# Weight quantisation and part of the row norm of a feed-forward placed inside the last units of the attention before it

## What is computed

```python
x = x + tanh(g_xattn[0]) * L0_xattn(ctx_1024, layernorm(x), mask, ...)   # latents attend to context and themselves
x = x + tanh(g_ffn[0])   * L0_ffn(layernorm(x), ...)                     # eight experts, two per row
x = x + tanh(g_xattn[1]) * L1_xattn(layernorm(x), ctx_1024, ...)         # 16 heads of 16
x = x + tanh(g_ffn[1])   * L1_ffn(layernorm(x), w_gate, w_up, w_down)
```

```python
def _weight_quant(w):
    scale = 1.0 / clip(mean(abs(w)), 1e-05)
    return clip(round(w * scale), -1.0, 1.0) / scale
def _act_quant(x):
    scale = 127.0 / clip(max(abs(x), axis=-1), 1e-05)
    return clip(round(x * scale), -128.0, 127.0) / scale
def _bitlinear(x, w):
    return einsum('bsi,oi->bso', _act_quant(x), _weight_quant(w))
def L1_ffn(x, w_gate, w_up, w_down):
    return _bitlinear(silu(_bitlinear(x, w_gate)) * _bitlinear(x, w_up), w_down)
```

## Time and profile before

| | |
|---|---|
| median of 3 runs | 3298.25 us (3297.76 to 3301.66) |
| profiled execution | 3298.45 us |
| its span in the trace | 3296.6 us |
| TensorE (PE) busy | 2955.8 us, 90% |
| VectorE (DVE) busy | 2432.6 us, 74% |
| ScalarE (ACT) busy | 1802.2 us, 55% |
| GpSimd (POOL) busy | 2106.7 us, 64% |
| mean granted TensorE clock | 0.968 |

### The profile page before, as it was taken

How to read it: one execution, slowest core, us unless ns; L and a number is a source line. 1 busy time by engine, 2 the same in 40 slices (tenths; PEclk the granted TensorE clock), 3 DMA queues, 4 the chain that set the end, 5 groups by cost and what they waited for, 6 DMA issues and landing times. The chain is left out here.

```text
span 3296.6 us, 53602 instructions
## 1 busy us (share of the span) xinstructions
PE 2955.8 (90%) x21720; PEld 1092.9 (33%) x21720; DVE 2432.6 (74%) x3016; ACT 1802.2 (55%) x2008; POOL 2106.7 (64%) x1000
## 2 busy tenths in 40 slices
PE   5899999999999999999999999996695899999947
PEld 3233333333333333333333333332562233332314
DVE  8777877677777678767777777872556888888658
ACT  4455455555455555545544554444442788888833
POOL 4787988898898888889789888898500211111022
PEclk9999999999999999999999999998897899999969
DMA  1000000000000000000000000000200100000000
GB/s 61 6 1 1 1 7 1 1 7 1 1 7 1 1 1 7 1 1 7 1 1 2 1 1 1 1 1 1 83 16 13 44 7 8 7 6 7 4 1 26
DMA packets 24616, 28.73 MB, mean 9 GB/s; under 512 B 6511, under 2 KB 21296, under 8 KB 24370
## 3 DMA queue, kind: packets, MB, share of 16 engines
q1 hardware_dynamic: 24370, 25.31, 2.6%
HBM read 17.42 MB, written 2.10 MB: 6 GB/s over the span
## 5 line engine op out<-in xcount | busy, mean ns | idle before, releaser
L460 POOL TENSOR_TENSOR a_acc<-a_acc,a_prob 128x1024 f32<-128x1024 f32 x704 | 1724.7, 2450 | 298.3 <-ACT a_prob L592 216.4
L710 DVE TENSOR_REDUCE a_part_max<-wide 128x2 f32<-128x1024 f32 x880 | 1069.3, 1215 | 442.1 <-PE wide L997 441.4
L592 ACT ACTIVATE a_prob<-slot,a_mask_bias 128x1024 f32<-128x1024 f32 x928 | 987.6, 1113 | 738.4 <-PE slot L1026 721.5
L1041 PE MATMUL bank<-a_prob,a_val 128*64 128x512 f32 x3712 | 896.8, 605 | 2.1 <-ACT a_prob L592 2.1
L1325 ACT ACTIVATE a_prob<-slot,a_mask_bias 128x1024 f32<-128x1024 f32 x416 | 455.4, 1116 | 66.7 <-PE slot L1483 53.7
L997 PE MATMUL wide<-a_k_hi,a_q_hi 64*128 64x512 f16 (+1 forms) x2016 | 352.6, 362 | 113.8 <-DVE a_part_max L710 106.1
L1367 DVE TENSOR_REDUCE a_part_max<-wide 128x1 f32<-128x512 f32 x514 | 333.3, 683 | 37.5 <-PE wide L1471 20.6
L1041 PEld LDWEIGHTS bank<-a_prob,a_val 128*64 128x64 f32 x3712 | 226.4, 136 | 393.7 <-issue 289.2
L1026 PE MATMUL slot<-a_q_hi,a_k_lo 64*128 64x512 f16 x1856 | 352.6, 377 | 0.0
L1026 PE MATMUL slot<-a_q_hi,a_k_step_hi 64*128 64x512 f16 x1728 | 328.1, 376 | 2.3 <-ACT a_prob L592 2.2
L1026 PE MATMUL slot<-a_q_lo,a_k_step_hi 64*128 64x512 f16 x1728 | 327.7, 376 | 0.0
(11 more groups left out here) (391 smaller groups left out, 3277.8 us busy)
## 6 DMA issues: line engine op xcount, KB each, us to landing
a_w_staged<-in_w SPq DMA_DIRECT2D x8, 384.0 KB, 3.2
x_res<-in_x SPq DMA_DIRECT2D x4, 512.0 KB, 5.7
a_q_op<-a_hi SPq DMA_DIRECT2D x128, 16.0 KB, 1.8
out_x<-x_res SPq DMA_DIRECT2D x16, 128.0 KB
a_k_op<-mid_k_hi SPq DMA_DIRECT2D x32, 52.0 KB, 2.2
mid_context<-in_ctxt SPq DMA_DIRECT2D x1, 1601.0 KB, 6.5
mid_w_staged<-in_w1a SPq DMA_DIRECT2D x4, 384.5 KB, 6.3
a_acc<-in_ctx SPq DMA_DIRECT2D x3, 512.0 KB, 8.3
```

The costliest lines, as they stand in the source:

```text
L460: nc.gpsimd.tensor_tensor(acc, before, prob[:, k % R, :], ALU.add).then_inc(added_p, 1)
L592: nc.scalar.activation(prob[:, k % R, :], m.slot[k % 2][:, :], ACT.Exp, bias=mbias[:, t:t + 1]).then_inc(probs_ready, 1)
L710: nc.vector.reduce_max(part_max[:, w % 2, :, j, c], pairs, AX.X).then_inc(max_used, 1)
L1041: ins = nc.tensor.matmul(av[r, :], val[g % 2][:, t, r], prob[:, k % R, h * QB:(h + 1) * QB], start=(t == 0), stop=(t == NT - 1), tile_posi ...
```

## The change

The stage of the row norm is gone, and `stage_norm` with it. `keep_for_quantised` reserves the feed-forward's tiles ahead of the second attention, and `stage_cross` gets them as `ffn`. On VectorE the sums over the weights stand at step 23 of unit 14; the scales and the first weight's quantisation at step 6 of unit 15; the other two at step 12; the measuring of row tiles 0 to 7 at step 18. Behind the last step VectorE measures tiles 8 to 11 and normalises tiles 0 to 11 ahead of `invert(last)`, and takes their row scales behind `divide(last)`. ScalarE takes the square root ahead of `take_raw(last)`. TensorE has the matmul for the mean at step 6 of unit 15. Tiles 12 to 15, those of the last block, are measured, normalised and scaled in the feed-forward's stage, on VectorE around `take_x(0)` and `take_x(1)`. GpSimd there starts without a wait. The normalised tiles 0 to 11 lie in the memory of the context's transposes (`m.ch`, `m.cl`), which nobody reads by then.

```diff
+        self.sum_at, self.mean_at, self.weights_at, self.rows_at = 23, 6, 12, 18
...
+                if w == a.units - 1 and s == a.mean_at:
+                    uses.append(("mean", 0))
...
+            act.wait_ge(rows_measured, 2)
+            deviate_rows(nc, ffn, 0, ffn.early).then_inc(rows_std, 1)
             take_raw(last)
...
+            def weight_sums():
+                dve.wait_ge(fetched, 16 * len(ahead_of_use))
+                nc.vector.memset(ffn.ones[:, :], 1.0)
+                nc.vector.memset(ffn.eps[:, :], EPS)
+                for n in range(3):
+                    ins = nc.vector.tensor_reduce(ffn.wsum[:, n:n + 1], ffn.wf[n][:, :], AX.X, ALU.add, apply_absolute_value=True)
+                ins.then_inc(wsum_done, 1)
+
+            def weight_scales():
+                dve.wait_ge(ring_ready, use_n["mean", 0] + 1)
+                nc.vector.tensor_scalar(ffn.wmean[:, :], bank(("mean", 0))[:, 0:3], 1.0 / (FF * D), 1e-5, ALU.mult, ALU.max).then_inc(ring_used, 1)
+                dve.wait_ge(ring_used, use_n["mean", 0] + 1)
+                nc.vector.tensor_scalar(ffn.gain[:, :], ffn.wmean[:, 2:3], m.tg[:, ffn.gate:ffn.gate + 1], None, ALU.mult)
+                link(nc.vector.reciprocal(ffn.wscale[:, :], ffn.wmean[:, :]))
...
+                    if w == last - 1 and s == a.sum_at:
+                        weight_sums()
+                    if w == last and s == a.mean_at:
+                        weight_scales()
+                        quantise_weight(nc, ffn, 0, link)
+                    if w == last and s == a.weights_at:
+                        quantise_weight(nc, ffn, 1, link)
+                        quantise_weight(nc, ffn, 2, link)
+                    if w == last and s == a.rows_at:
+                        dve.wait_ge(res_added, 2 * (last - 1))
+                        measure_rows(nc, m, ffn, 0, 8, link).then_inc(rows_measured, 1)
+            dve.wait_ge(res_added, 2 * last)
+            measure_rows(nc, m, ffn, 8, ffn.early - 8, link).then_inc(rows_measured, 1)
+            dve.wait_ge(rows_measured, 2)
+            dve.wait_ge(rows_std, 1)
+            norm_rows(nc, m, ffn, 0, ffn.early, link)
             invert(last)
             divide(last)
+            scale_rows(nc, ffn, 0, ffn.early, link).then_inc(rows_scaled, 1)
+            dve.wait_ge(rows_scaled, 1)
...
+            def mean():
+                free_bank(("mean", 0))
+                pe.wait_ge(wsum_done, 1)
+                nc.tensor.matmul(bank(("mean", 0))[:, 0:3], ffn.ones[:, :], ffn.wsum[:, :], start=True, stop=True).then_inc(ring_ready, 1)
...
+                    if w == last and s == a.mean_at:
+                        mean()
...
+    early = [part[:, :, :].rearrange("p c k -> p (c k)").bitcast(FP32) for part in (m.ch, m.cl)]
+    q.xn = [early[t // 6][:, t % 6 * D:(t % 6 + 1) * D] for t in range(NX - 4)]
...
+    q.early = NX - 4
...
+def quantise_weight(nc, q, n, link):
+    w = q.wf[n][:, :]
+    link(nc.vector.tensor_scalar(w, w, q.wscale[:, n:n + 1], ROUND, ALU.mult, ALU.add))
+    link(nc.vector.tensor_scalar(w, w, ROUND, 1.0, ALU.subtract, ALU.min))
+    link(nc.vector.tensor_scalar(q.wq[n][:, :], w, -1.0, None, ALU.max))
...
+def measure_rows(nc, m, q, t0, n, link):
+    for t in range(t0, t0 + n):
+        ins = nc.vector.bn_stats(q.stats[:, t, :], m.x[:, t, :])
+    link(ins)
+    for t in range(t0, t0 + n):
+        ins = nc.vector.bn_aggr(q.mv[:, t, :], q.stats[:, t, :])
+    return ins
+
+
+def deviate_rows(nc, q, t0, n):
+    return nc.scalar.activation(q.std[:, t0:t0 + n], q.mv[:, t0:t0 + n, 1], ACT.Sqrt, bias=q.eps[:, 0:1])
...
+def norm_rows(nc, m, q, t0, n, link):
+    link(nc.vector.reciprocal(q.rstd[:, t0:t0 + n], q.std[:, t0:t0 + n]))
+    for t in range(t0, t0 + n):
+        ins = nc.vector.tensor_scalar(q.xn[t], m.x[:, t, :], q.mv[:, t, 0:1], q.rstd[:, t:t + 1], ALU.subtract, ALU.mult)
+    link(ins)
...
+def scale_rows(nc, q, t0, n, link):
+
+    r = slice(t0, t0 + n)
+    for t in range(t0, t0 + n):
+        ins = nc.vector.tensor_reduce(q.amax[:, t:t + 1], q.xn[t], AX.X, ALU.max, apply_absolute_value=True)
+    link(ins)
+    link(nc.vector.tensor_scalar(q.amax[:, r], q.amax[:, r], 1e-5, None, ALU.max))
+    link(nc.vector.reciprocal(q.ascale[:, r], q.amax[:, r]))
+    nc.vector.tensor_scalar(q.ascale[:, r], q.ascale[:, r], 127.0, None, ALU.mult)
+    link(nc.vector.tensor_scalar(q.adq[:, r], q.amax[:, r], 1.0 / 127.0, None, ALU.mult))
+    nc.vector.tensor_scalar(q.gs[:, r], q.adq[:, r], q.wmean[:, 0:1], None, ALU.mult)
+    return nc.vector.tensor_scalar(q.us[:, r], q.adq[:, r], q.wmean[:, 1:2], None, ALU.mult)
...
-            nc.vector.memset(ones[:, :], 1.0)
-            for n in range(3):
-                ins = nc.vector.tensor_reduce(wsum[:, n:n + 1], wf[n][:, :], AX.X, ALU.add, apply_absolute_value=True)
...
+            measure_rows(nc, m, q, q.early, NX - q.early, link).then_inc(late_measured, 1)
             take_x(0)
             take_x(1)
+            dve.wait_ge(late_std, 1)
+            norm_rows(nc, m, q, q.early, NX - q.early, link)
+            scale_rows(nc, q, q.early, NX - q.early, link).then_inc(rows_ready, 1)
+            dve.wait_ge(rows_ready, 1)
...
-            pool.wait_ge(scales_ready, 1)
             for t in range(NX):
                 if t >= 2:
...
+                if t == q.early:
+                    pool.wait_ge(rows_ready, 1)
+                nc.gpsimd.tensor_scalar(xi[:, t % 2, :], q.xn[t], q.ascale[:, t:t + 1], ROUND, ALU.mult, ALU.add).then_inc(xi_part, 1)
...
-            act.wait_ge(scales_ready, 1)
+            act.wait_ge(late_measured, 1)
+            deviate_rows(nc, q, q.early, NX - q.early).then_inc(late_std, 1)
...
-            pe.wait_ge(wsum_done, 1)
-            nc.tensor.matmul(m.bank[0][:, 0:3], ones[:, :], wsum[:, :], start=True, stop=True).then_inc(wmean_done, 1)
...
-                        pe.wait_ge(wq_done, n + 1)
-                    else:
+                    if t:
...
+            ffn = keep_for_quantised(nc, m, ctx)
...
-            with nc.sbuf_tensor("xn_rows", [P, NX, D], FP32) as rows:
-                stage_norm(nc, m, "nx3", m.x, NX, rows=rows)
-                stage_quantised(nc, m, rows, 3, wf, out)
...
+            stage_quantised(nc, m, ffn, out)
```

More of the change, by code:

```diff
@@ L2135, in _, with keep_for_quantised, sb @@
                 turn(1, b)
-def stage_quantised(nc, m, xn, gate, wf, out):
+def keep_for_quantised(nc, m, ctx):
+    def sb(name, shape, dt=FP32):
+        return ctx.enter_context(nc.sbuf_tensor(f"ffn_{name}", shape, dt))
+    q = Memory()
+    q.gate = 3
+    q.wf = [sb(f"w{n}", [P, FF * DC]) for n in range(3)]
+    q.wq = [sb(f"wq{n}", [P, FF * DC], BF16) for n in range(3)]
+    q.ones = sb("ones", [P, P])
+    early = [part[:, :, :].rearrange("p c k -> p (c k)").bitcast(FP32) for part in (m.ch, m.cl)]
+    q.xn = [early[t // 6][:, t % 6 * D:(t % 6 + 1) * D] for t in range(NX - 4)]
+    q.wsum, q.wmean, q.wscale, q.gain = sb("wsum", [P, 3]), sb("wmean", [P, 3]), sb("wscale", [P, 3]), sb("gain", [P, 1])
+    q.stats, q.mv, q.std, q.rstd, q.eps = sb("stats", [P, NX, 6]), sb("mv", [P, NX, 2]), sb("std", [P, NX]), sb("rstd", [P, NX]), sb("eps", [P, 1])
+    q.amax, q.ascale, q.adq = sb("amax", [P, NX]), sb("ascale", [P, NX]), sb("adq", [P, NX])
+    q.gs, q.us = sb("gate_scale", [P, NX]), sb("up_scale", [P, NX])
+    q.early = NX - 4
+    return q
@@ L2143, in stage_quantised @@
+def stage_quantised(nc, m, q, out):
     KF = FF // P
@@ L2146, in sb @@
             return ctx.enter_context(nc.sbuf_tensor(f"ffn_{name}", shape, dt))
-        wq = [sb(f"wq{n}", [P, 2048], BF16) for n in range(3)]
-        ones = sb("ones", [P, P])
-        wsum, wmean, wscale = sb("wsum", [P, 3]), sb("wmean", [P, 3]), sb("wscale", [P, 3])
-        amax, ascale, adq = sb("amax", [P, NX]), sb("ascale", [P, NX]), sb("adq", [P, NX])
-        gain = sb("gain", [P, 1])
-        gs, us = sb("gate_scale", [P, NX]), sb("up_scale", [P, NX])
+        wq = q.wq
+        late = sb("xn", [P, 4, D])
+        q.xn += [late[:, t, :] for t in range(4)]
         xi = sb("xi", [P, 2, D])
@@ L2255, in _ @@
         def _(act):
[L2256 removed]
+            act.wait_ge(late_measured, 1)
+            deviate_rows(nc, q, q.early, NX - q.early).then_inc(late_std, 1)
             for t in range(NX):
                 act.wait_ge(gate_ready, t + 1)
+                if t == q.early:
+                    act.wait_ge(rows_ready, 1)
                 if t >= 2:
                     act.wait_ge(h_done, t - 1)
[L2261 removed]
+                nc.scalar.activation(sg[:, t % 2, :], m.slot[0][:, :], ACT.Silu, scale=q.gs[:, t:t + 1]).then_inc(silu_done, 1)
                 if t:
```

148 lines of the change are left out of this document (17 added, 131 removed).

## The result

The changed kernel takes **3268.87 us** (median of 4 runs, 3268.37 to 3270.92), against 3298.72 for the kernel before in runs that alternate with it. The ratio is 0.9911, 95% interval 0.9900 to 0.9923: 29.9 us less. The forecast was 3266.8 in a range of 3263 to 3271.

What follows compares the result with a forecast made beforehand. VectorE was taken to bound the last feed-forward loop and to work nearly alone before it; h of tile 0 moving from 3204.83 to 3173.15 saves 31.7 us, so 3298.45 becomes 3266.8, range 3263 to 3271.

Steps and rivals of the forecast that it cites:

- Sums, mean, first weight: hidden.: Last attention units: weight sums, mean matmul and first weight's passes fit idle time at cost 0, reciprocal spare about 0.1 us.
- The other weights, the measuring: hidden.: Last attention unit: second and third weight (8.1 us) and measuring rows 0 to 11 end before ScalarE's last exponential, hidden.
- Deviation +0.43: End of attention: square root with table load on ScalarE delays the copy of the last values by 0.43 us.
- Normalising ahead of the last reciprocal +2.93: End of attention: twelve normalisations on VectorE delay the last softmax's reciprocal by 2.93 us, the deviation's 0.43 included.
- The clock falls before the spread.: TensorE idles before the last spread and drops to 1.2 GHz: spread to division about 2.05 us, outputs 3.7.
- Stage end.: Attention's end: GpSimd ends last near 3163.4 (+5.3 us), hiding VectorE's row scales at 3162.7; next stage starts at 3164.4.
- h of tile 0: First product of the feed-forward's last loop, expected at 3173.15 instead of 3204.83, set by VectorE's row scales.
- my rival of chance 0.06: New stage: VectorE's late normalisations wait for GpSimd on tile 2, +0.95 us, so 3267.7; chance 0.06.
- My other road, through Silu: New stage: gate matmuls, then 4.5 us to Silu's end, table load included, 8.35 us behind the stage's start.
- The loop unchanged.: Feed-forward's last sixteen-tile loop, VectorE's: untouched by the change, still 5.3 us a tile.
- The clock rises later in the loop: Rival: 3 to 7 us more at 1.2 GHz slow tiles 0 to 2, giving 3267.5 to 3271; chance 0.06.
- the held softmax: Rival: first weight's passes delay unit 14's reciprocal, TensorE stands at the spread; 3267.6 to 3269.4; chance 0.12.

Runs made afterwards that it cites:

- fill_gap: Changed kernel plus twelve matmuls without use in TensorE's idle time between the last denominators and the spread; 3266.99 us.
- weights_only: Changed kernel with only the weights' sums and quantisation left in the attention, all sixteen row tiles back in the feed-forward's stage; 3281.06 us.
- norm_split_fill: Changed kernel with the twelve normalisations split in fours around last reciprocal and division, plus matmuls without use in TensorE's waits of tiles 0 and 1; 3263.23 us.
- after_again: The changed kernel run and profiled a second time with no edit; median 3270.00 us.
- after: First profile of the changed kernel, no further edit; median 3268.87 us.
- after_third: Third profile of the changed kernel, no edit; a single execution of 3268.49 us.
- invert_first: Changed kernel with VectorE's last reciprocal and division ahead of the norm of row tiles 0 to 11; 3271.20 us.

## Why the prediction was right

Step by step, against the changed kernel's profile:

- **Sums, mean, first weight: hidden.** Right. The mean fitted TensorE's gap (the scores behind it start 11.01 us behind the mark, before 11.02), and the reciprocal of unit 14 had 0.11 us to spare, with the handover of 0.14 us counted; I had 0.1.
- **The other weights, the measuring: hidden.** Right. One of the passes took 2.19 us instead of 1.23 beside GpSimd's addition; there VectorE waited, where I had expected GpSimd to be slowed. Nobody waited for it.
- **Deviation +0.43.** Measured +0.28: the copy started 35.81 us behind the mark, before 35.53.
- **Normalising ahead of the last reciprocal +2.93.** Measured 40.27 against 37.34: +2.93.
- **The clock falls before the spread.** Right: from the spread's start to the division 1.99 us, forecast 2.05; outputs 3.75, forecast 3.7. fill_gap shows that the gap did it and that without it h of tile 0 comes 1.4 us earlier.
- **Stage end.** Forecast: GpSimd at 49.3 behind the mark, VectorE at 48.6. Measured 49.3 and 49.5. One small scale of VectorE took 1.11 us beside GpSimd's last addition, so that VectorE ended last. The barrier then took 1.2 us, not 1.0.
- **h of tile 0.** Forecast 59.1 behind the mark, measured 59.6. The late normalisations took 1.75 us for four tiles beside GpSimd; in weights_only, where GpSimd waits, the same four took 1.37. That is my rival of chance 0.06, come true at 0.4 us and not at the 0.95 that I gave it. My other road, through Silu, was 1.4 us too long (Silu ended at 3170.16, 7.0 us behind the stage's start, forecast 8.35), mainly since the table load of 1.28 us did not stand in it; that did not matter, as VectorE's row scales came last.
- **The loop unchanged.** This is the step that failed: "Nothing in the change touches this loop". Its code is the same, its first tiles' timing is not, and it lost 2.5 to 2.6 us to TensorE's clock in all three profiles. By my own list, gaps in the loop's first tiles were a sign of being wrong, and they are there. I had a rival near it ("The clock rises later in the loop", chance 0.06, 3267.5 to 3271); its cost fits, its mechanism does not. The clock rose early, 1.4 to 2.2 us ahead of h of tile 0 (4.5 us behind it before), and fell again in or behind TensorE's waits for VectorE in the first tiles; norm_split_fill, which fills these waits, has the loop back at 79.2 us.

The forecast of 31.7 us is off by 0.6 for h0 and by 2.5 for the loop: 28.6 by the mark. The medians differ by 29.9 in this series and by 27.0 in the later one. So part of the closeness of 3268.87 to 3266.8 is luck of the runs. My forecast by itself had 3265.8 to 3267.8, and the result lies outside that; it lies in the range of 3263 to 3271 because I had widened that for the clock and the held softmax. The path up to h of tile 0 was right; the loop was not. Nor does one kernel repeat to better than 1.4 us behind the mark: in after_again the part behind h of tile 15 took 11.2 us, in after and after_third 12.7, and in it TensorE's clock fell 4.3 us later.

## What to carry to other kernels

Work can go into an engine's idle time at no cost as long as the one instruction queued behind it is still in time; find that instruction and its margin (here 0.11 us, the handover counted) before choosing the place. Towards the end of a stage the order on the engine decides: what another engine waits for goes first, and what has to wait for GpSimd (here the normalisations) goes where GpSimd is still. And a loop is not unchanged because its code is: look at when TensorE waits and how its clock stands in the first iterations.

## What was not expected of the hardware

VectorE waits for GpSimd, not only the other way round. The second six normalisations of 128x256 in invert_first took 4.21 us beside two of GpSimd's additions (1.47 and 1.50 us, else 1.28), the first six 2.03 without; a pass over 128x2048 took 2.19 beside one, 1.23 without; a scale on 12 columns took 1.11 beside one, 0.23 without. Row maxima (`TENSOR_REDUCE`, 2.05 us for six) took the same beside GpSimd as alone. This agrees with the Trainium skill (SBUF — State Buffer, "SBUF: two separate sides"), where the shared port pair is held for a whole instruction and "the other fully blocks". I had argued from their pace of 0.33 us that small normalisations need not be of the kind that meets GpSimd; they wait like the others.

TensorE's clock rose while it worked at 1.2 GHz without pause, and the engine then waited in each of the first tiles. In after it was back at 1.2 GHz in the wait of 2.20 us, for ten microseconds; in after_again it held through a wait of 1.88 us and fell behind the next (1.98 us), for seven. That the waits are the cause is shown by norm_split_fill alone, one profile, where matmuls without use in three waits held the clock.

ScalarE's table load for Silu ran at 3165.36, 3.7 us ahead of the activation that needs it, right behind the square root and not behind that activation's wait. In the kernel before it stood behind the wait and was on the path with 1.28 us.
